# Vision tower on one core: new orders of the work on TensorE, ScalarE and GpSimd, and a split first step of the FFN

## The reference

```python
# tokenizer: 36 patches of 16x16x3 = 768 pixels per image
h = layernorm(patches) * ln1_w + ln1_b
h = layernorm(h @ W + b) * ln2_w + ln2_b          # 768 -> 192
h = concat([cls, h], axis=1) + pos                # 37 tokens
# state-space block, with its own rms norm and residual
z  = layernorm(h);  xn = gamma * z / (rms(z) + 1e-6)
xc = causal_conv4(xn @ W_in.T + b_in, conv_w)      # 192 -> 384
s_t = sigmoid(A) * s_(t-1) + sigmoid(Bp) * xc_t;  y_t = sum_n(s_t * sigmoid(C))
h = h + (y @ W_out.T + b_out) + z
# FFN
n = layernorm(h)
patch tokens (31 an image): gelu(n @ W1 + b1) @ W2 + b2      # hidden 768
class tokens (6 an image):  a first-layer expert, a second-layer expert, softmax gate with top 1 mask
out = h + concat([class outputs, patch outputs])
```

## Time and profile before

| | us |
|---|---|
| median of 3 runs | 98.13 (97.84 to 98.38) |
| the profiled execution | 99.03 |
| its span | 97.3 |
| TensorE busy | 85.5 (88%) |
| VectorE busy | 60.9 (63%) |
| GpSimd busy | 41.1 (42%) |
| ScalarE busy | 38.7 (40%) |

### The profile page before, as it was taken

The page is one execution under the profiler, slowest core; times in us unless marked ns, Lnnn a source line. Parts: engine busy times, 40 slices in busy tenths (PEclk is TensorE's granted clock), DMA queues, the critical chain, the costliest instruction groups (busy, mean ns, idle before and its releaser), DMA issues.

```text
span 97.3 us, 1841 instructions
## 1 busy us (share of the span) xinstructions
PE 85.5 (88%) x579; PEld 71.0 (73%) x579; DVE 60.9 (63%) x209; ACT 38.7 (40%) x105; POOL 41.1 (42%) x112
## 2 busy tenths in 40 slices
PE   5997599999988978969999989969899999999940
PEld 5995399989966758757588889956577726888830
DVE  4659999547999999999976993573100307038410
ACT  0620957562345644104492053420964204870000
POOL 6525799998974230538746005353500400000000
PEclk9999999999999999999999999999999999999996
DMA  1999998497628994699999921010202100000211
GB/s 14 262 259 255 257 275 150 87 259 175 194 67 268 322 214 136 109 281 235 246 326 314 292 68 41 17 46 13 78 20 81 34 28 11 0 0 0 63 52 39
DMA packets 16294, 13.59 MB, mean 140 GB/s; under 512 B 5907, under 2 KB 14332, under 8 KB 16284
## 3 DMA queue, kind: packets, MB, share of 16 engines
q1 hardware_dynamic: 14860, 13.39, 52.0%
q10 hardware_dynamic: 1424, 0.08, 1.2%
HBM read 12.43 MB, written 1.04 MB: 138 GB/s over the span
## 4 chain that ended last, share of the span: by engine, by line
PE 55%; DVE 24%; DMA 7%; ACT 4%; ACTq 3%; issue 3%; DVEq 0%
PE ps L1184 50%; DMA ssm<-in_L_attn_C_dram 7%; DVE h L994 3%; DVE xT_area L1027 2%; DVE xs L1012 2%; DVE xT_area L1030 2%; PE ps L1208 2%; DVE st L1000 2%; DVE h L977 2%; DVE st L967 2%; ACT x4TT L654 2%; DVE xT_area L1036 1%; ACT xT_area L654 1%; DVE ag L969 1%; DVE Y L1036 1%
## 5 line engine op out<-in xcount | busy, mean ns | idle before, releaser
L1184 PE MATMUL ps<-W_area,xT_area 128*108 128x192 f32 (+2 forms) x72 | 13.7, 329 | 1.5 <-ACT xT_area L654 1.3
L1184 PEld LDWEIGHTS ps<-W_area,xT_area 128*108 128x108 f32 (+2 forms) x72 | 10.9, 170 | 2.3 <-issue 2.1
L1184 PE MATMUL ps<-W_sb,pixel_area 128*124 128x192 f32 x48 | 8.8, 332 | 0.0
L1184 PEld LDWEIGHTS ps<-W_sb,pixel_area 128*124 128x124 f32 x48 | 7.7, 187 | 1.2 <-issue 1.2
L1184 PE MATMUL ps<-WoutT,xT_area 128*108 128x192 f32 (+1 forms) x42 | 7.6, 328 | 1.0 <-DVE xT_area L1036 1.0
L1184 PEld LDWEIGHTS ps<-WoutT,xT_area 128*108 128x108 f32 (+1 forms) x42 | 6.8, 177 | 1.4 <-DVE xT_area L1036 1.4
L1184 PE MATMUL ps<-dM,WinT 128*128 128x216 f32 (+2 forms) x36 | 7.2, 335 | 0.0
L1184 PE MATMUL ps<-x4TT,W_sb 128*128 128x248 f32 x24 | 6.1, 387 | 1.1 <-ACT x4TT L654 1.1
L654 ACT ACTIVATE xT_area<-ps,ln_col 128x576 f32<-128x576 f32 (+1 forms) x6 | 4.9, 809 | 4.5 <-PE ps L1208 4.5
L1184 PEld LDWEIGHTS ps<-dM,WinT 128*128 128x128 f32 x36 | 5.8, 190 | 0.8 <-issue 0.8
L1184 PE MATMUL ps<-warm_sb 128*128 128x128 f32 x24 | 5.4, 412 | 1.1 <-DVE warm_sb L863 1.1
(11 more groups left out here) (212 smaller groups left out, 197.3 us busy)
## 6 DMA issues: line engine op xcount, KB each, us to landing
line_area<-in_L_ffn_A_W_dram SPq DMA_DIRECT2D x5, 576.0 KB, 9.4
A_sb<-in_L_ffn_A_W_dram SPq DMA_DIRECT2D x5, 384.0 KB, 4.3
pixel_area<-in_x_dram SPq DMA_DIRECT2D x6, 288.0 KB, 7.1
A1R<-in_L_ffn_A_W_dram SPq DMA_DIRECT2D x10, 96.0 KB, 3.6
W_area<-in_L_tok_W_dram SPq DMA_DIRECT2D x2, 288.0 KB, 5.6
W_sb<-in_L_ffn_moe_W_dram SPq DMA_DIRECT2D x1, 576.0 KB, 8.2
W_sb<-in_L_ffn_moe_W_dram SPq DMA_DIRECT2D x1, 384.0 KB, 5.9
W1R<-in_L_ffn_moe_W_dram SPq DMA_DIRECT2D x2, 192.0 KB, 5.7
```

The costliest lines, as they stand in the source:

```text
L1184: return t.matmul(out_, lhsT, rhs, start=start, stop=stop, skip_group_check=True)
```

## The change

It touches the instruction lists of four places.
- TensorE, tokenizer and state-space block: the products of the tokenizer are in a new order: step 0 whole before `turn(1)`, step 2 whole, steps 3 to 5 by pairs of groups; the last products of groups 4 and 5 and their fold stand behind `transform(0)`. K's transposition moves behind `transform_rest(0)`, K's transform behind the first half of `project_in_pair(0)`, which is split into `project_in_even` and `project_in_odd`. W_out's parts 0 and 1 are transposed behind `project_in_odd(0)`, into bank 5. The product for `ob` stands behind `project_out(1)` and `transform(4)`.
- ScalarE: the first Sqrt (with its table load) and the gamma loads move back, WoutT 0 and 1 are copied behind `K2` and ahead of `roots3(3)`, `put_x4T(1)` ahead of `put_P(4)`.
- GpSimd: `add_cls` ahead of `root2(5)`.
- `x4bank(1)` is in bank 5, so that `turn_x4(1)` follows `turn_x4(0)` at once; `project_out(4)` waits for its copy. In the FFN the first step's products are split by columns into groups 0 to 2 and group 3 (`up_first`), the rests of steps 0 and 1 follow step 1's products, and gates and the first layers of three experts stand ahead of step 2.

The diff, with unchanged lines mostly left out and eight columns of indent removed:

```diff
@@ -330,6 +330,8 @@
 def x4bank(g):
+    if g == 1:
+        return ps[:, 5, 256:512].rearrange("p (s c) -> p s c", s=2)
     return ps[:, 6 if g == NG - 1 else 0, :].rearrange("p (s c) -> p s c", s=2)
...
@@ -624,8 +626,8 @@
     residual_scales(3)
+    add_cls()
     root2(5)
-    add_cls()
     add_ob(0)
...
@@ -684,22 +686,22 @@
     a_.activation(ssm[:, :, :, :], ssm[:, :, :, :], ACT.Sigmoid).then_inc(sig_ready, 1)
-    a_.activation(table_row[:, 1:2], ones[:, 0:1], ACT.Sqrt)
     put_xT(1)
-    act.dma_start(gcol[:, 0:1], gamma[0:DL].unsqueeze(1)).then_inc(l_gam, 16)
-    for i in range(2):
-        act.dma_start(gcol[DR * i:DR * (i + 1), 1:2], gamma[DL:D].unsqueeze(1)).then_inc(l_gam, 16)
     line_up(2)
     put_xT(2)
+    a_.activation(table_row[:, 1:2], ones[:, 0:1], ACT.Sqrt)
     act.wait_ge(t_gT, 1)
...
     put_xT(3)
+    act.dma_start(gcol[:, 0:1], gamma[0:DL].unsqueeze(1)).then_inc(l_gam, 16)
+    for i in range(2):
+        act.dma_start(gcol[DR * i:DR * (i + 1), 1:2], gamma[DL:D].unsqueeze(1)).then_inc(l_gam, 16)
     put_xT(4)
+    put_xT(5)
     act.wait_ge(var1, 1)
...
     a_.activation(ms1[:, :, 2], ms1[:, :, 1], ACT.Sqrt, bias=eps5[0:BH, :]).then_inc(rs1_ready, 1)
-    put_xT(5)
     act.wait_ge(l_gam, 48)
...
@@ -754,10 +756,8 @@
     act.wait_ge(t_w, 3)
-    copy(WoutT[:, 0:2, :], ps[:, 6, 0:2 * D].rearrange("p (e d) -> p e d", e=2)).then_inc(wT_ready, 1)
+    copy(WoutT[:, 2, :], ps[:, 3, 0:D]).then_inc(wT_ready, 1)
     roots3(1)
-    act.wait_ge(t_w, 4)
-    copy(WoutT[:, 2, :], ps[:, 3, 0:D]).then_inc(wT_ready, 1)
     act.wait_ge(t_K, 1)
...
@@ -770,6 +770,8 @@
              scale=(1.0 if s else -1.0) / S).then_inc(Kh_ready, 1)
+    act.wait_ge(t_w, 4)
+    copy(WoutT[:, 0:2, :], ps[:, 5, 0:2 * D].rearrange("p (e d) -> p e d", e=2)).then_inc(wT_ready, 1)
     roots3(3)
...
@@ -821,8 +823,8 @@
     put_x4T(0)
+    put_x4T(1)
     put_P(4)
-    put_x4T(1)
     put_P(5)
...
@@ -1248,46 +1250,39 @@
     warm(WARM2)
-    product(0, [0, 1, 2])
+    product(0, [0, 1, 2, 3, 4, 5])
     turn(1)
-    product(0, [3, 4, 5])
+    pe.wait_ge(tab_ready, 1)
+    t.transpose(ps[0:2 * S, 6, 0:128], tb_n.rearrange("p s f -> p (s f)"), ident[:, :]).then_inc(t_gT, 1)
     product(1, [0, 1, 2])
...
-    pe.wait_ge(tab_ready, 1)
-    t.transpose(ps[0:2 * S, 6, 0:128], tb_n.rearrange("p s f -> p (s f)"), ident[:, :]).then_inc(t_gT, 1)
     product(1, [3, 4, 5])
     turn(3)
-    product(2, [0, 1, 2, 3])
+    product(2, [0, 1, 2, 3, 4, 5])
     turn(4)
-    product(3, [0, 1, 2, 3])
     turn(5)
+    product(3, [0, 1])
     product(4, [0, 1])
+    product(5, [0, 1])
...
     turn_Win()
-    product(5, [0, 1])
-    product(2, [4, 5])
+    product(3, [2, 3])
     pe.wait_ge(rows_ready, 1)
...
     fold([0, 1])
-    product(3, [4, 5])
+    product(4, [2, 3])
     turn_Win_rest()
-    product(4, [2, 3])
     product(5, [2, 3])
...
     fold([2, 3])
+    product(3, [4, 5])
     pe.wait_ge(l_Wout, 32)
-    pe.wait_ge(wT_ready, 2)
-    turn_Wout(0, 6, 0)
-    turn_Wout(1, 6, D).then_inc(t_w, 1)
     turn_Wout(2, 3, 0).then_inc(t_w, 1)
-    product(4, [4, 5])
-    product(5, [4, 5])
-    fold([4, 5])
...
@@ -1307,7 +1302,7 @@
         if p == 0:
-            pe.wait_ge(wT_ready, 4)
+            pe.wait_ge(wT_ready, 3)
         elif p == 1:
...
@@ -1337,7 +1332,8 @@
-    def project_in_pair(p):
+    def project_in_even(p):
...
@@ -1353,7 +1349,9 @@
             project_in_rest(g + 1, i)
-        project_in(g + 1)
+    def project_in_odd(p):
+        project_in(2 * p + 1)
...
@@ -1366,6 +1364,8 @@
             pe.wait_ge(dR_ready, 3)
+        if g == 4:
+            pe.wait_ge(x4T_ready, 2)
         for j, (pair, c0, n) in enumerate(PTILES[g]):
...
@@ -1401,6 +1401,8 @@
             pe.wait_ge(dM_ready, 3)
+        elif g == 1:
+            pe.wait_ge(Psb_ready, 3)
         elif g < NG - 1:
...
@@ -1409,44 +1411,53 @@
     transform(0)
+    product(4, [4, 5])
+    product(5, [4, 5])
+    fold([4, 5])
+    transform(1)
+    transform_rest(0)
     pe.wait_ge(K_ready, 1)
-    pe.wait_ge(wT_ready, 3)
+    pe.wait_ge(wT_ready, 2)
     for e in range(ET):
...
     ins.then_inc(t_K, 1)
-    transform(1)
-    transform_rest(0)
+    project_in_even(0)
     pe.wait_ge(KT_ready, 1)
...
     ins.then_inc(t_Kh, 1)
-    project_in_pair(0)
+    project_in_odd(0)
+    pe.wait_ge(h_free, 4)
+    turn_Wout(0, 5, 0)
+    turn_Wout(1, 5, D).then_inc(t_w, 1)
     transform(2)
...
     project_out(0)
-    project_in_pair(1)
+    project_in_even(1)
+    project_in_odd(1)
+    project_out(1)
+    transform(4)
     pe.wait_ge(u_ready, 2)
...
     ins.then_inc(t_ob, 1)
-    project_out(1)
-    transform(4)
     invert(0)
...
     invert(1)
-    project_in_pair(2)
+    project_in_even(2)
+    project_in_odd(2)
     project_out(3)
+    turn_x4(0)
+    turn_x4(1)
     invert(2)
-    turn_x4(0)
     project_out(4)
-    turn_x4(1)
     invert(3)
...
@@ -1454,15 +1465,24 @@
-    def up(s, js, last):
+    def up(s, js):
         for j in js:
...
             mm(upslot(s, j), W1_sb[:, m * 128:(m + 1) * 128], x4TT[:, 0, b0:b0 + nb, NCLS:T], j < 2, False)
-        if not last:
-            return
+    def up_first():
+        for b0, nb, n in ((B0[0], NBG[0] + NBG[2], 3), (B0[3], NBG[3], 4)):
+            pe.wait_ge(x4T_ready, n)
+            for j in range(4):
+                m = STEPS[0][j][1]
+                mm(upslot(0, j)[:, NPT * b0:NPT * (b0 + nb)], W1_sb[:, m * 128:(m + 1) * 128],
+                   x4TT[:, 0, b0:b0 + nb, NCLS:T], j < 2 and n == 3, False)
+    def up_rest(s):
         for j in range(4):
...
@@ -1482,36 +1502,45 @@
+    def gates():
+        pe.wait_ge(l_G, 32)
+        pe.wait_ge(xc_ready, NG)
+        pe.wait_ge(h3_ready, NG)
+        mm(ps[0:CT, 0, 0:2 * NCLS], c_main[:, 0:CT], GL.rearrange("p i j -> p (i j)"),
+           True, False)
+        pe.wait_ge(xRc_ready, NG)
+        pe.wait_ge(const_ready, 5)
+        mm(ps[0:CT, 0, 0:2 * NCLS], c_rest[:, 0:CT], GR.rearrange("p i j -> p (i j)"),
+           False, True).then_inc(t_g, 1)
+    def first_layers_lo():
+        pe.wait_ge(l_A1, 16 * 3 * NEXP)
+        pe.wait_ge(Psb_ready, NG)
+        pe.wait_ge(pads_ready, 4)
+        for k in range(2):
+            for a in range(NLO):
+                mm(ps[32 * a:32 * a + 32, 6 + k, 0:HH], c_main[:, 32 * a:32 * a + 32],
+                   A1_sb[:, a, k * HH:(k + 1) * HH], True, False)
     pe.wait_ge(l_W1, 48)
-    up(0, [0, 1, 2, 3], True)
+    up_first()
     turn_x4(4)
...
     pe.wait_ge(h3_ready, NG)
-    up(1, [0, 1], False)
-    up(1, [2, 3], True)
+    up(1, [0, 1, 2, 3])
+    up_rest(0)
+    up_rest(1)
+    gates()
+    first_layers_lo()
     pe.wait_ge(hid_ready, 4)
-    up(2, [0, 1, 2, 3], True)
+    up(2, [0, 1, 2, 3])
+    up_rest(2)
     pe.wait_ge(l_W2, 16)
...
-    pe.wait_ge(l_G, 32)
-    pe.wait_ge(xc_ready, NG)
-    pe.wait_ge(h3_ready, NG)
-    mm(ps[0:CT, 0, 0:2 * NCLS], c_main[:, 0:CT], GL.rearrange("p i j -> p (i j)"),
-       True, False)
-    pe.wait_ge(xRc_ready, NG)
-    pe.wait_ge(const_ready, 5)
-    mm(ps[0:CT, 0, 0:2 * NCLS], c_rest[:, 0:CT], GR.rearrange("p i j -> p (i j)"),
-       False, True).then_inc(t_g, 1)
-    pe.wait_ge(l_A1, 16 * 3 * NEXP)
-    pe.wait_ge(Psb_ready, NG)
-    pe.wait_ge(pads_ready, 4)
-    for k in range(2):
-        for a in range(NLO):
-            mm(ps[32 * a:32 * a + 32, 6 + k, 0:HH], c_main[:, 32 * a:32 * a + 32],
-               A1_sb[:, a, k * HH:(k + 1) * HH], True, False)
...
```

## The result

| | before | after |
|---|---|---|
| median of 4 runs, us | 97.98 (97.37 to 98.38) | 102.62 (101.22 to 103.64) |
| the profiled execution | 99.03 | 101.22 |
| its span | 97.3 | 99.5 |
| TensorE busy | 85.5 | 86.2 |
| VectorE busy | 60.9 | 60.1 |

The change makes the kernel slower: ratio 1.0397, 95% interval 1.0256 to 1.0539. The time, 102.6 us, is above the range of 99.0 to 101.6. The four executions of the changed kernel, with the mean granted clock of TensorE in each (1 is 2.4 GHz throughout), already say where to look: 101.22 (0.997), 102.42 (0.983), 102.81 (0.983), 103.64 (0.983). The one that was profiled is the one at 0.997.

What follows compares the result with a forecast made beforehand. Bound by TensorE to 22.49 us, VectorE to 47.18, then TensorE. +2.6 at transform(5), +0.1 for project_out(4)'s wait and -0.6 in the FFN gave +2.1, hence 100.2 us against the 98.13 median; range 99.0 to 101.6.

Steps and rivals of the forecast that it cites:

- the collision of 1.13: VectorE's tokens(5) waiting for u_rep: add_cls ahead of root2(5) was to end it, -0.7 us.
- The FFN: End of kernel: TensorE's 1.1 us of waits for x4T shrink, less the column split's cost; gain 0.6 us.
- the split: FFN's first step: dividing products of 248 columns into 186 and 62 was to cost 0.3 us.
- The drain of 1.38 us: ScalarE's table load: the skill's added cost, 1.4 us on the total; not seen in the row, so not used.
- the rival Clock: TensorE's clock falls to 1.2 GHz behind idle pieces of 2 us, doubling project_in's 3.3 us: up to 103.4; chance 0.08.
- so a matmul costs after the change what a row shows now: All TensorE work: clock stays at 2.4 GHz whenever it works, so earlier durations were used unchanged.
- the reference of the sum: Whole kernel: +2.1 us, worked out against the 99.03 us profiled execution, was applied to the median of 98.13.
- The gain of 0.85 us in the front: Up to fold 0: earlier product 1 starts VectorE's block at 21.65 us, 0.85 earlier.
- The price of the middle: VectorE waits about 3 us ahead of normed(3) for roots3(3); multiply(0) starts at 37.45 instead of 34.38, +3.1 us.
- the rival Gamma late: Front: gamma loads take 6.7 us, land at 22.1 and cost 0.7 us, total 100.9; chance 0.07.
- So they cost nothing: Front: moved gamma loads land at 20.0 us, before WinT's copy at 20.25, so add 0 us.

Runs made afterwards that it cites:

- e1: Changed kernel with ScalarE's roots3(3) moved ahead of its wait for K's transform, so ahead of kr, K2 and the W_out copy: 102.4 us, 100.26 at full clock.
- e2: Changed kernel with K's transform back ahead of project_in_even(0) and roots3(3) ahead of the W_out copy: 98.96 us, ratio 1.0069.
- e7: e2 with ScalarE's roots3(5) and put_P(1) also moved ahead of the copy of ob: 97.45 us, ratio 0.993.
- e8: Changed kernel with 6 dummy TensorE products ahead of transform(0) only: 103.2 us, ratio 1.0501.
- e4: Changed kernel, same order, with 21 dummy products filling five idle places of TensorE: 101.7 us, ratio 1.0363.
- e10: Changed kernel with transform(2), transform(3) and their rest held until multiply(0) is done, joining TensorE's idle pieces: 106.34 us, ratio 1.0742.
- e9: Changed kernel with 4 dummy products ahead of transform(3) and 5 ahead of project_out(0) only: 102.41 us, ratio 1.0408.
- e6: Kernel before with only the change's FFN order (up_first, up_rest, gates and experts): 97.52 us, ratio 0.9934.
- e11: Kernel before with e6's FFN, add_cls ahead of root2(5), ob's product behind transform(4), roots3(5) and put_P(1) ahead of ob's copy: 96.64 us, ratio 0.9854.
- e5: Kernel before with only the change's TensorE and ScalarE order up to the third fold, W_out's transposes left in place: 98.22 us, ratio 1.0008.

## Why the prediction was right and where it failed

**Right, by its steps.** Product 1 at 11.19 (given 11.35), fold 0 at 20.62 (20.7), first statistics at 21.56 (21.65). K2's copy ends at 35.53 (35.6). VectorE idles 3.15 us ahead of `normed(3)`, released by the roots (about 3), and `multiply(0)` starts at 37.28 (37.45). TensorE waits 0.93 us for dM, from 30.12 (30.1). Line L996 never takes longer than 0.43 us now (the collision of 1.13 gone), P(1), behind the copy of `ob`, ends at 48.70 (49.05), and `transform(5)` starts at 49.61 (49.75). The FFN gives -0.65 us (-0.6): the 16 instructions of `up_first` take 2.17 us to the next row (68.64 - 66.47), eight of 248 columns in step 2 take 1.90 (77.16 - 75.26), so the split costs 0.27 (0.3). The span grew by 2.2 us (+2.1). e1, e2 and e7 undo the three locks one by one and get from 101.3 us at full clock to 100.3, some 98.9 and some 97.3, so this mechanism is shown. An agreement within 0.2 us in the front is partly luck: in the ten traces with the new front product 1 starts anywhere from 10.52 to 11.44. The drain of 1.38 us behind the table load that the Trainium skill gives (ScalarE: Activation LUTs, What ACT_TABLE_LOAD costs) isn't there: the load starts at 13.81, takes 1.28, and the next ACTIVATE starts at 15.10.

**Failed: the rival Clock, at 0.08.** The prediction named it, with the right place, 38 to 40 us, and gave it 8 chances in 100. It came in 3 of 4 executions, then in 5 of 6, and so sets the median: 101.2 to 101.4 us at full clock became 102.6 and 103.0. The step that failed is "so a matmul costs after the change what a row shows now", from the earlier trace rows; and that the trace before keeps 2.4 GHz over an idle piece of up to 1.3 us was taken to say that this is safe. It speaks of one such piece with full work around it, and of one execution. The change puts 1.28 and 1.39 us of idle time around one microsecond of products, and further pieces (1.62, 0.93, 1.07) around these. The price was too high instead: 3.3 us (100.2 + 3.3 is 103.5, given as 103.4), for products at half speed throughout, where e8 shows 1.6 in one fall; the executions at 0.983 lie 0.8 to 2.4 us above the one at full clock beside them. e4 (no fall in six, with the same waits on VectorE) against the changed kernel (8 of 10) and e10 (4 of 4) shows that idle time of TensorE is the cause, and e8's trace shows one place. Which of the pieces are needed stays open: e9 filled the ones at 36 to 40 us and four of six executions still ran at 0.98.

**Failed: the reference of the sum.** The gain of 0.85 us in the front was read as the difference to the profiled execution of before, and the whole sum was then carried over to the median, 0.9 us lower. But the 0.9 us of that execution lay in the same stretch. The text asked why the copy ahead of product 1 starts at 11.30 and found the table load of 9.90; it did not ask what that load is queued behind. It is the sigmoid, whose input had landed late, and e6, with the same front, starts product 1 0.72 us and `multiply(0)` 0.78 us earlier. Against such a front the change starts `multiply(0)` 37.28 - 33.60 = 3.7 us later (3.4 against e11's 33.92), where the two profiled executions differ by 2.9. The price of the middle was right: from the first `xs` to `multiply(0)` it is 11.4 us now and 7.5 in the traces of before and e6, +3.9, and the text had +3.1 with the 0.85 of the front taken off. The term that failed is that 0.85. By the spans: e6 has 95.8 us and the changed kernel 99.5, both with the new FFN, so +3.7 without it and +3.1 with its 0.65 counted, where the text had +2.1. This alone moves 100.2 to 101.2. (The trace after starts late too, with product 0 at 7.48 against 6.69 in e5, 6.81 in e7 and 6.82 in e6, but at most 0.2 of that is left at the first `xs`: 25.87, against 25.73 in e5 and 25.68 in e7.) e5 confirms it from the other side: the new front alone measures 1.0008 (0.9974 to 1.0043).

**Failed: gamma.** The last load was to land at 20.0 and WinT's copy to start at 20.25; it starts at 21.29, with the loads issued from 15.11 to 16.03 and up to 5.2 us under way. This is the rival Gamma late, at 0.07, which looked for its price on TensorE alone. "So they cost nothing" was true of TensorE's `turn_Win_rest` in the trace after (22.01, given 22.05), while in e1, e2 and e9 TensorE waits 0.53, 0.21 and 0.30 us there, and it was not true of ScalarE's queue: the copies and the roots behind the wait come late, and e5 shows 0.45 us of the front's lead lost between the first statistics and the first `xs`. The change frees product 1 from one early load and binds the first `xs` to another. That gamma alone takes the whole gain of the front is argued from the rows; no run has the new front with the loads issued early.

Of the sum of errors, 102.6 - 100.2 = 2.4 us, the reference is about 1.0 (what part of it is the late gamma is not separated) and the clock, in the median, about 1.4 (102.6 - 101.2).

## What to carry to other kernels

A profiled execution that isn't the median must be asked where it lost its time before a gain is subtracted from it; where the change shortens that very stretch, the sum belongs against a usual front. A load that is issued later than before needs the cover up to everything queued behind its first user, here up to VectorE's first reciprocal, and not only up to that user. When a new order makes an in-order engine stop, the idle time that this leaves on TensorE can have a price of its own, here in 8 of 10 executions, and a trace at full clock doesn't show it: compare the mean clock of every execution. And a wait on a shared in-order queue (ScalarE's `t_Kh`, `t_w`, `t_ob` here) should stand behind every short operation that another engine is waiting for: opening the three locks turned +4.5% into -0.7%, not counting the three of twelve executions in which the clock fell.

## What the runs showed of the hardware

- With idle pieces of 1.28 and 1.40 us and about one microsecond of products between them, the granted clock went from 1.00 to 0.50 right behind them in e8's trace and stayed up in the trace after, with the same order and nearly the same times. The number of executions with a mean clock of 0.983 or less: 8 of 10 for the changed kernel, 6 of 6 for e8, 4 of 6 for e9, 4 of 4 for e10, 3 of 4 for e1, 2 of 9 for e2, 3 of 12 for e7, none of 6 for e4.
- Behind one piece of 2.18 us ahead of product 1 the clock fell to 0.50 in the kernel before; behind 1.12, 1.32 and 1.52 us at the same place (e6, before, e11) it did not.
- The start of a load's first user varies by 0.8 us between executions of one front (8.84 to 9.66 us in four traces), and passes on in full through product 1, 2.72 or 2.73 us later. The three small gamma loads, issued behind `put_xT(3)`, release their first user between 20.92 and 22.00 us in ten traces.
- At the start of the kernel the pace of TensorE differs between executions. The first six transposes take 0.96 us to the next row in the trace after (5.54 to 6.50) and 0.52 us in e5's (5.07 to 5.59), though the granted clock is recorded as 1.00 from 3 to 7 us in both. Product 0 starts at 7.48 and 6.69 us in these two. The clock line doesn't show it; the rows do.
- The ScalarE table load takes 1.28 us and the next ACTIVATE starts 0.01 us behind it (13.81, 15.10).
